# Cross attention and expert-choice FFN on one core: the rows of the third plain column turned by DMA, and two pair turns queued ahead of the weights

## The reference

```
x = x + xattn(layernorm(x), ctx, Wq, Wk, Wv, Wo, bo)
xn = layernorm(x)
scores = einsum('ntd,ed->nte', xn, gate_w); probs = softmax(scores)
g, m = top_k(probs.transpose(0, 2, 1), k)      # k = 2.0 * 2048 / 8 = 512 tokens per expert and batch
xin = xn[batch_idx, m]
h = gelu(einsum('nekd,edf->nekf', xin, w1))    # 512 -> 2048
h = einsum('nekf,efd->nekd', h, w2)            # 2048 -> 512
x = x + zeros.at[batch_idx, m].add(g * h)
```

## Time and profile before

| | us |
|---|---|
| median of 3 runs | 1667.96 (1666.43 to 1668.12) |
| the profiled run's own time | 1667.86 |
| its span, first to last instruction | 1665.7 |
| PE busy | 1647.2 (99%) |
| DVE busy | 1103.0 (66%) |
| ACT busy | 942.7 (57%) |
| mean granted TensorE clock | 0.996 |

### The profile page before, as it was taken

How to read it: one execution, slowest core, us unless ns; L and a number is a source line. 1 busy time by engine, 2 the same in 40 slices (tenths; PEclk the granted TensorE clock), 3 DMA queues, 4 the chain that set the end, 5 groups by cost and what they waited for, 6 DMA issues and landing times.

```text
span 1665.7 us, 23177 instructions
## 1 busy us (share of the span) xinstructions
PE 1647.2 (99%) x8508; PEld 1407.7 (85%) x8508; DVE 1103.0 (66%) x1992; ACT 942.7 (57%) x2045; POOL 304.3 (18%) x364
## 2 busy tenths in 40 slices
PE   9999999999999999999999999999999999999997
PEld 9999999877888887888888888888888888888886
DVE  7555697877766648655775576558655855686663
ACT  5678777744332556456646654666466546654441
POOL 3233233111122110300140023003300320040002
PEclk9999999999999999999999999999999999999999
DMA  3243436354334473512451244234423432342004
GB/s 134 77 142 111 152 128 222 120 152 127 127 77 164 129 176 111 129 26 76 135 118 26 77 141 111 46 88 120 101 76 90 96 93 77 101 96 57 26 1 51
DMA packets 134917, 171.06 MB, mean 103 GB/s; under 512 B 62701, under 2 KB 63881, under 8 KB 134809
## 3 DMA queue, kind: packets, MB, share of 16 engines
q1 hardware_dynamic: 120441, 136.04, 25.9%
q0 software_dynamic: 14336, 33.56, 10.7%
q10 hardware_dynamic: 32, 0.03, 0.0%
HBM read 121.38 MB, written 33.55 MB: 93 GB/s over the span
## 4 chain that ended last, share of the span: by engine, by line
PE 94%; DMA 2%; ACT 2%; DVE 1%; issue 0%; POOL 0%; POOLq 0%; SPq 0%; ACTq 0%; DVEq 0%
PE ps L2218 10%; PE ps L2216 10%; PE ps L2217 10%; PE ps L2196 9%; PE ps L2195 9%; PE ps L2194 9%; PE ps L1229 4%; PE ps L1230 4%; PE ps L1231 4%; PE ps L2131 3%; PE ps L2118 3%; PE ps L2120 3%; PE ps L2119 3%; PE ps L2132 3%; PE ps L2133 3%; DMA turned_planes<-planes 1%
## 5 line engine op out<-in xcount | busy, mean ns | idle before, releaser
L2216 PE MATMUL ps<-v2h,hhS 128*128 128x512 f32 x768 | 298.8, 389 | 0.0
L2218 PE MATMUL ps<-v2h,hlS 128*128 128x512 f32 x768 | 298.8, 389 | 0.0
L2217 PE MATMUL ps<-v2l,hhS 128*128 128x512 f32 x768 | 298.8, 389 | 0.0
L2195 PE MATMUL ps<-Tl,Wh 128*128 128x512 f32 x672 | 261.4, 389 | 0.0
L2196 PE MATMUL ps<-Th,Wl 128*128 128x512 f32 x672 | 261.4, 389 | 0.0
L2194 PE MATMUL ps<-Th,Wh 128*128 128x512 f32 x672 | 261.4, 389 | 0.0
L1598 POOL DMA_INDIRECT out_dram<-YS,tok_idx x48 | 105.0, 2187 | 816.2 <-DVE YS L2027 805.0
L2027 DVE SCALAR_TENSOR_TENSOR YS<-ps,tok_gate,YS 128x512 f32<-128x512 f32 x144 | 106.4, 748 | 120.0 <-PE ps L2218 120.0
L1771 ACT ACTIVATE v2h<-w_raw 128x512 fp32r<-128x512 f32 x96 | 57.4, 622 | 215.7 <-PE ps L2218 215.7
L2217 PEld LDWEIGHTS ps<-v2l,hhS 128*128 128x128 f32 x768 | 144.2, 188 | 30.0
L2216 PEld LDWEIGHTS ps<-v2h,hhS 128*128 128x128 f32 x768 | 144.2, 188 | 29.9
(11 more groups left out here) (284 smaller groups left out, 3599.2 us busy)
## 6 DMA issues: line engine op xcount, KB each, us to landing
w_raw<-in_L_ffn_w_dram SPq DMA_DIRECT2D x80, 1024.0 KB, 7.2
XB<-in_x_dram SPq DMA_DIRECT2D x16, 512.0 KB, 4.1
XR<-in_x_dram SPq DMA_DIRECT2D x16, 512.0 KB, 6.3
out_dram<-X SPq DMA_DIRECT2D x16, 512.0 KB, 5.0
xn_rows<-XN SPq DMA_DIRECT2D x16, 512.0 KB, 5.3
w_raw<-in_L_xattn_Wq_dram SPq DMA_DIRECT2D x1, 1024.0 KB, 9.1
wo_sb<-in_L_xattn_Wo_dram SPq DMA_DIRECT2D x2, 512.0 KB, 11.5
w_raw<-in_L_xattn_Wk_dram SPq DMA_DIRECT2D x1, 768.0 KB, 6.0
```

The lines of the kernel that those rows point to most:

```text
L2195: nc.tensor.matmul(ps[:, bank, :], wh, tl, start=False, stop=False, **go_on)
L2216: nc.tensor.matmul(ps[:, bank, :], th, wh, start=(t == 0), stop=False)
L2217: nc.tensor.matmul(ps[:, bank, :], th, wl, start=False, stop=False)
L2218: last = nc.tensor.matmul(ps[:, bank, :], tl, wh, start=False, stop=(t == GF - 1))
```

## The change

Column 2 is turned by DMA as well. Its two splits both come in step 13 of column 1 (slot 29), its joins in steps 14 and 15 (slots 30 and 31), and all four chunks in step 15. The 16 transposes on PE in slots 27 to 30 and their copies are gone. On SP its two transposing DMAs stand behind the load of weight group 9. For columns 1 and 3 the first chunk is made one step later (step 14 in place of 13). For the two pair keys the transposing DMAs, which stood on SP behind the loads of weight groups 14 and 15, now stand ahead of them. Three semaphores of the sums `TT1`, `TT2`, `TT4` become one with counts.

```diff
-        TURNED = ((1,), (3,), (0, 1), (0, 0)) + tuple((x, b) for x in range(1, NS) for b in range(B))
+        TURNED = ((1,), (2,), (3,), (0, 1), (0, 0)) + tuple((x, b) for x in range(1, NS) for b in range(B))
...
-        SPLIT_AT, WORDS_AT, CHUNKS_AT = (10, 11), (12, 13), {13: (0,), 14: (1,), 15: (2, 3)}
+        SPLIT_AT = {i: {13: (0, 1)} if i == 1 else {10: (0,), 11: (1,)} for i in range(3)}
+        WORDS_AT = {i: {14: (0,), 15: (1,)} if i == 1 else {12: (0,), 13: (1,)} for i in range(3)}
+        CHUNKS_AT = {i: {15: (0, 1, 2, 3)} if i == 1 else {14: (0, 1), 15: (2, 3)} for i in range(3)}
...
         def sp_experts(sp):
             for gg in range(2, G * len(PLAIN)):
-                sp_weights(sp, gg)
-                if gg in (G, 3 * G):
-                    for a in range(2):
-                        sp_turn(sp, (gg // G,) if gg == G else (3,), a)
                 if gg >= 4 * G - 2:
                     for a in range(2):
                         sp_turn(sp, (0, 4 * G - 1 - gg), a)
+                sp_weights(sp, gg)
+                if gg in (G, 2 * G + 1, 3 * G):
+                    for a in range(2):
+                        sp_turn(sp, (gg // G,), a)
...
-                    pool.wait_ge(s_Td, x)
+                    pool.wait_ge(s_Td, 3 * x)
...
-                k = turn(n - 1)
-                if k is not None:
-                    act_token_chunk(act, (n - 1) // KF + 1, k, 6)
                 i, f = divmod(n, KF)
                 if (i + 1,) in TURNED:
-                    if f == SPLIT_AT[0]:
+                    for a in SPLIT_AT[i].get(f, ()):
                         act.wait_ge(f_rows, 16 * CT * (i + 2))
-                    if f in SPLIT_AT:
-                        act_split((i + 1,), SPLIT_AT.index(f))
-                    if f in WORDS_AT:
-                        act_words(act, (i + 1,), WORDS_AT.index(f))
-                    for k in CHUNKS_AT.get(f, ()):
+                        act_split((i + 1,), a)
+                    for a in WORDS_AT[i].get(f, ()):
+                        act_words(act, (i + 1,), a)
+                    for k in CHUNKS_AT[i].get(f, ()):
                         act_turned_chunk(act, i + 1, k)
...
-                k = turn(n - 1)
-                if k is not None:
-                    dve_token_chunk(dve, (n - 1) // KF + 1, k, 6)
...
-                if turn(n) is not None:
-                    pe_token_chunk(pe, n // KF + 1, turn(n), 6)
```

More of the change, by code:

```diff
@@ L1491, in xattn_expert_choice @@
         s_raw2 = [sem(f"s_raw2_{i}") for i in range(2)]
-        (s_prod, s_u1, s_c11, s_u2, s_u7, s_c22, s_c21, s_gelu, s_hid, s_sum, s_Wh, s_Wl, s_v2h, s_v2l, s_dn, s_ev, s_Ta, s_Tb, s_T1,
-         s_T2, s_Td, s_Th, s_Tl, s_scat) = (sem(f"s_{n}") for n in (
-             "prod u1 c11 u2 u7 c22 c21 gelu hid sum Wh Wl v2h v2l dn ev Ta Tb T1 T2 Td Th Tl scat").split())
+        (s_prod, s_u1, s_c11, s_u2, s_u7, s_c22, s_c21, s_gelu, s_hid, s_sum, s_Wh, s_Wl, s_v2h, s_v2l, s_dn, s_ev, s_Ta, s_Tb,
+         s_Td, s_Th, s_Tl, s_scat) = (sem(f"s_{n}") for n in (
+             "prod u1 c11 u2 u7 c22 c21 gelu hid sum Wh Wl v2h v2l dn ev Ta Tb Td Th Tl scat").split())
         s_rows = [sem(f"s_rows{b}") for b in range(B)]
@@ L1516, in xattn_expert_choice @@
         VALS_AT = CHOICE_AT + 4
-        TURNS_1 = tuple(range(KF // 2 + 3, KF - 1))
         HOTS = [q for q in range(VALS_AT + 1, 3 * KF + 4)
@@ L1523, in xattn_expert_choice @@
         found_of = {q: m for m, q in FOUND_AT.items()}
-        def turn(n):
-            i, f = divmod(n, KF)
-            return TURNS_1.index(f) if i == 1 and f in TURNS_1 else None
         def sp_experts(sp):
             for gg in range(2, G * len(PLAIN)):
-                sp_weights(sp, gg)
-                if gg in (G, 3 * G):
-                    for a in range(2):
-                        sp_turn(sp, (gg // G,) if gg == G else (3,), a)
                 if gg >= 4 * G - 2:
@@ L1646, in act_token_chunk @@
         def act_token_chunk(act, i, k, bank):
-            act.wait_ge(f_tr, i // 2 * KD + k + 1)
+            act.wait_ge(f_tr, i * KD + k + 1)
             nc.scalar.activation(eTh[i % 2][:, k, :], ps[:, bank, :], ACT.Copy).then_inc(f_eTh, 1)
@@ L1743, in t_high @@
                     if idx == TT3:
-                        act.wait_ge(s_T1, x + 1)
+                        act.wait_ge(s_Td, 3 * x + 1)
                     elif idx == TT2:
-                        act.wait_ge(s_T2, x + 1)
+                        act.wait_ge(s_Td, 3 * x + 2)
                     elif idx == TT4:
-                        act.wait_ge(s_Td, x + 1)
+                        act.wait_ge(s_Td, 3 * (x + 1))
                     nc.scalar.activation(Th[:, idx], Tf[:, idx], ACT.Copy).then_inc(s_Th, 1)
@@ L1944, in t_sum @@
                 elif idx == TT1:
-                    nc.vector.tensor_tensor(Tf[:, TT1], x1, x0, ALU.subtract).then_inc(s_T1, 1)
+                    nc.vector.tensor_tensor(Tf[:, TT1], x1, x0, ALU.subtract).then_inc(s_Td, 1)
                 elif idx == TT2:
-                    dve.wait_ge(s_T1, x + 1)
-                    nc.vector.tensor_tensor(Tf[:, TT2], x1b, Tf[:, TT1], ALU.subtract).then_inc(s_T2, 1)
+                    dve.wait_ge(s_Td, 3 * x + 1)
+                    nc.vector.tensor_tensor(Tf[:, TT2], x1b, Tf[:, TT1], ALU.subtract).then_inc(s_Td, 1)
                 else:
-                    dve.wait_ge(s_T2, x + 1)
+                    dve.wait_ge(s_Td, 3 * x + 2)
                     nc.vector.tensor_tensor(Tf[:, TT4], x0b, Tf[:, TT2], ALU.subtract).then_inc(s_Td, 1)
```

## The result

The changed kernel took 1657.26 us (median of 4 runs, 1657.01 to 1659.1), the kernel before 1667.79 (4 runs, 1666.43 to 1668.12, the three of the table above among them). The ratio is 0.9945, 95% interval 0.9929 to 0.9960: faster by 0.4 to 0.7%, and 0.55% of 1667.8 is 9.2 us. Forecast were 8.24 us and 1659.6, with a range of 1658.0 to 1666.5. The ratio times the 1667.96 of before is 1658.8, inside the range; the bare median is 0.7 us under its low end. The profiled run of the changed kernel took 1659.1.

The account below looks back on a forecast made before the run. The prediction took PE to bound the kernel, busy 1647.2 of 1665.7 us. It summed 1.78 + 6.46 + 0 = 8.24 us less, 1667.86 - 8.24 = 1659.6 us, with a range of 1658.0 to 1666.5.

Parts of the forecast that it names:

- Pair turns: Near 625 us: PE's 3.62 us stop for a late gelu and 2.84 us of lower clock behind it go, 6.46 us won.
- "4 to 7 us" for key (0, 1): Sign of being right: the pair keys' transposing DMAs land 4 to 7 us after issue.
- the bound of 13.0: Worst landing time of a pair key's transposing DMA in the old trace, in us from issue, used as upper bound.
- the bound of 619.8: Latest time, in us, at which ACT's join of key (0, 0) may begin without stopping PE.
- the clock's part: Behind PE's stop near 625 us: 14 matmul steps at the lower clock of 1.2 GHz cost 2.84 us more.
- Rival (b): PE's stop goes but the clock's fall stays, set off by another short stop: 5.4 us won, 1662.5 us; chance 0.09.
- That the weights alone held the DMA back: Key (0, 0)'s DMA, issued just behind 2 MB of weights on SP, took 10.7 us against 4.3 with nothing queued.
- Transposes: Slots 27 to 30: four blocks of four transposes gone from PE, some 0.45 us each, 1.78 us won.
- Column 2's new wait: Slots 29 to 32: column 2's DMA lands behind group 9 at 478.6 us, before PE needs it; cost 0.
- the 3.15 us behind the weights: Delay of key (0, 0)'s DMA landing after the weights' in the old trace, reused for column 2's landing behind group 9.
- its slack of 0.3: Column 2's DMA may land as late as 478.9 us before PE's lookup waits for the one-hot table; 478.6 was taken.
- "The first chunk one step later: 0": Columns 1 and 3: first chunk done in step 14 of 16 and read two steps on, so cost 0.

Follow-up runs that it names:

- e1: Kernel before with only the two pair turns put ahead of the loads of weight groups 14 and 15: 1661.02 us, ratio 0.9970.
- e2: Changed kernel with the pair turns put back behind the weight loads: 1663.83 us, ratio 0.9984 to the kernel before.
- e8: Changed kernel with GpSimd's scatter of column 2 held until key (0, 1) has been turned: 1657.64 us, ratio 0.9946 to the kernel before.
- e3: Changed kernel with the first chunk of columns 1 and 3 in step 13 again: 1659.18 us, ratio 0.9958 to the kernel before.
- e4: Changed kernel with column 2's turn on SP ahead of weight group 9: 1657.96 us, ratio 0.9949 to the kernel before.
- e5: Changed kernel with column 2's splits in slot 30 and both joins in slot 31: 1660.63 us, ratio 0.9960 to the kernel before.
- e7: Changed kernel with column 2's splits in slot 30, both joins in slot 31, the first join made three times: 1666.98 us, ratio 1.0002 to the kernel before.
- e6: Changed kernel with column 2's splits in slot 30, both joins in slot 31, the first join made twice: 1664.67 us, ratio 0.9986 to the kernel before.

## Why the prediction was right, and where a size was off

**Pair turns: 6.46 us forecast, 6.48 read.** Reading the stop and the clock as one price held: e1 wins both with that edit alone, e2 brings both back. The forecast that the key (0, 0) would land in 4.3 us and the group behind it in time held too (4.2 and 4.3 us, no wait of PE). Wrong was "4 to 7 us" for key (0, 1): 8.1 and 11.5, the scatter's doing (e8), inside the bound of 13.0 that the working had kept. So group 14 went out at 598.63, 5 us later than I had it, and key (0, 0) at 607.85, 3 us later; the bound of 619.8 for its join carried that. What was lucky is the size of the clock's part. It is 1.73, 2.50, 2.61 and 2.86 us in four traces, so the term was good to 1 us at best; it hangs on when the clock falls, in the stop or behind it (e2). Rival (b), that the fall would stay without the stop, is out: neither the changed kernel nor e1, e3 and e4 have one there. That the weights alone held the DMA back, as the prediction has it, stays open for some 1.5 us (the hole, under e5).

**Transposes: 1.78 forecast, 1.95 read.** The step mis-sized is where I stopped counting: at the second matmul behind a block. The matmuls after it in the kernel before still follow at 0.231 and not 0.227 us:

```profile
472.75 0.39 PE L2119 MATMUL ps<-eTl,w1h 128*128 128x512 f32 x1
...
475.06 0.39 PE L2120 MATMUL ps<-eTh,w1l 128*128 128x512 f32 x1
```

10 steps in 2.31 us where 2.27 were due, 0.04 for each block (the other three take 2.30 to 2.31) and 0.16 for four. By the durations it would have been 4.3 us: the starts were the right thing to read. By the figure of the Trainium skill (TensorE: Matmul & The Clock Gate, Part 4: PE-mode transpose) it would have been an estimated 4.4 us; the trace has 1.95.

**Column 2's new wait: 0 forecast, 0 read.** The landing was forecast at 7.4 us from the issue and was 6.3. The term mis-sized is the 3.15 us behind the weights: group 9 landed at 467.31 + 7.7 = 475.0 and the transpose at 477.0, 2.0 us behind. The 3.15 were read where the hole of 1.5 us stands (see e5), which may be the difference. The chain behind it came out link by link. With the landing 1.1 us sooner than the prediction took, its slack of 0.3 should be 1.4 us. Read are the join on ACT and the table on DVE:

```profile
477.14 2.65 ACT L1482 ACTIVATE XB<-turned_planes 128x512 uint16<-128x512 uint16 x4 [2.86 <-DMA turned_planes<-planes]
```

```profile
486.95 2.28 DVE L777 TENSOR_TENSOR hot<-row,col_iota 128x2048 bf16<-128x2048 f32 x1
```

The table ends at 489.2, and the lookup starts at 490.32, where it was due: 1.1 us of slack. With the ring order that the Trainium skill states (DMA: Bandwidth & Descriptors, Queues, rings and completion order) the landings agree, 2.0 us behind the weights and 4.4 us from the issue in e4; no run here tells it from a sharing of the DMA engines.

**"The first chunk one step later: 0" was wrong, by 0.96 us** by the table and 0.97 by the experiment (e3). I priced the moved chunk by when it is read next, and not by what stands behind it on DVE. The wait stands among PE's waits of the kernel before, beside the earlier trace rows, and I had passed it over as small:

```profile
PE ps L686 <- DVE cnt L680: 1.0, 2, 0.8
```

Together, with 0.17 and 0.02 for the two terms above: 8.24 + 0.96 + 0.19 = 9.39 us against 9.2 by the ratio. The medians are 10.5 us apart; against the later runs of the kernel before (medians 1666.49 and 1666.9) it is 9.2 and 9.6. What is left is not explained by the change; the attention part alone varies by 2.2 us between profiles, and the interval of the ratio is 5.2 us wide.

No kernel here beats the changed one clearly: e4 and e8 (1657.96 and 1657.64) remove waits that PE does not see. In the plain part PE's waits are down to one of 0.2 us.

## What to carry to other kernels

A queue's order is part of the schedule: a transfer that somebody waits for soon belongs ahead of one that has slots of time, also where it makes the second one wait for the first one's producers. When an instruction is moved, look at what stands behind it on its engine, in the old place as in the new; the reader of its result is only half the question. And price a stop of TensorE with the clock behind it: here stops of 3.6 to 6.7 us cost 1.7 to 2.9 us more, about half of the time worked at the lower clock, and two stops of 1.3 and 1.0 us nothing.

## What the runs showed of the hardware

- Idle stretches of PE of 3.46, 3.56, 3.91 and 6.52 us each came with a granted clock of half (1.2 GHz), begun in the stop or, for the 3.56, some 0.5 us behind it; idle stretches of 1.29 and 0.95 us did not (e5). The price of the fall, 1.73 to 2.86 us, did not grow with the stop.
- A transposing DMA of half a column's rows lands in 4.2 to 4.8 us undisturbed, in 6.3 with 2 MB of weights issued some 4 us ahead of it on its queue, in 10.7 with them 1 us ahead and a fetch of instructions, and in 6.8 to 11.6 with GpSimd's scatter on another queue (the changed kernel, e1 and e3 to e7).
- In e5 the transposes moved 11 GB/s for 1.5 us, between 175 and 200, around one fetch of instructions; both landed after 6.0 to 6.1 us. In the kernel before all queues together moved 13 GB/s for 1.5 us, with transposes waiting and 283 and 288 on either side, again at one fetch. No run isolates the fetch.
- Matmul no. 2100, in the attention part that is the same in all kernels, starts anywhere between 273.2 and 275.4 us. A lower clock also came without an idle stretch: in the changed kernel's profile it was 0.57 from 31 to 35 us with PE busy, there and in the 6 us before. The profiles of e5, e6 and e8 have the same, the other six do not:

```profile
31.00:35.00 4.00, 4.00 (x19) 4.00 (x19) 3.53 (x10) 2.53 (x6) 1.49 (x3) 0.57 0.00 0
```
